# A delta-rule attention whose outputs move from VectorE's recurrence to tiles of 128 tokens on TensorE

## The reference, cut to what matters

```python
def _step(Sm, inputs):                       # Sm: 16x16 per sequence and head
    q_t, k_t, v_t, beta_t = inputs
    Sk = einsum('bhde,bhe->bhd', Sm, k_t)
    delta = v_t - Sk
    Sm = Sm + beta_t[..., None] * einsum('bhd,bhe->bhde', delta, k_t)
    o_t = einsum('bhde,bhe->bhd', Sm, q_t)
    return (Sm, o_t)
# k is divided by its norm; 512 steps, for 16 x 16 = 256 (sequence, head) pairs
x = x + outputs @ Wo + bo
```

## Time and profile before

| what | value |
|---|---|
| three runs | 5764.4, 5775.8, 5776.9 us; median 5775.8 |
| the profiled execution | 5775.2 us, its span 5773.9 us |
| TensorE busy | 3437.4 us (60%), weight loads 2437.2 us (42%) |
| VectorE busy | 4123.4 us (71%) |
| ScalarE busy | 1977.3 us (34%) |
| GpSimd busy | 1477.9 us (26%) |
| TensorE's granted clock, mean | 0.79 of full speed |
| memory traffic | 593.45 MB by DMA, 103 GB/s in the mean |

### The profile page before, as it was taken

One profiled execution on the slowest core, in us unless ns is written; L12 is line 12 of the kernel. 1 busy time (PEld: TensorE's weight loads), 2 busy tenths in 40 slices (PEclk: granted clock), 3 DMA queues, 4 the chain that ended last, 5 costly groups with the idle time before them and its releaser, 6 DMA issues.

```text
span 5773.9 us, 72351 instructions
## 1 busy us (share of the span) xinstructions
PE 3437.4 (60%) x21396; PEld 2437.2 (42%) x21396; DVE 4123.4 (71%) x10439; ACT 1977.3 (34%) x4743; POOL 1477.9 (26%) x1736
## 2 busy tenths in 40 slices
PE   6322153573436534163458888866888589867864
PEld 3101132353314423153436655644666256644654
DVE  1999988999899988998356656664666366655423
ACT  3111021231113311031236555644565255634432
POOL 2010013303451133503450212034000620044334
PEclk8555566796768966597679989978999689978977
DMA  1210001452215511363432334322333243333577
GB/s 48 115 42 6 0 20 47 131 168 71 72 52 168 149 59 57 105 190 115 149 115 87 103 118 127 97 70 96 99 97 91 101 121 98 94 113 119 172 221 210
DMA packets 429264, 593.45 MB, mean 103 GB/s; under 512 B 57680, under 2 KB 304080, under 8 KB 428752
## 3 DMA queue, kind: packets, MB, share of 16 engines
q1 hardware_dynamic: 379728, 454.55, 26.3%
q0 software_dynamic: 49152, 134.28, 7.0%
HBM read 378.89 MB, written 209.72 MB: 102 GB/s over the span
## 4 chain that ended last, share of the span: by engine, by line
DVE 40%; PE 34%; issue 10%; POOL 7%; ACT 4%; DMA 3%; another core or an unknown queue 1%; SPq 1%; DVEq 0%; ACTq 0%; POOLq 0%
PE psum L1019 6%; DVE rec L1083 5%; DVE rec L1085 4%; DVE skb L1088 4%; DVE rec L1096 4%; DVE rec L1099 4%; DVE region L1091 3%; PE psum L929 3%; PE psum L874 3%; PE psum L1027 3%; POOL xbuck L1661 2%; PE psum L913 2%; DVE psum L1201 2%; POOL yg L1671 2%; PE psum L915 2%
## 5 line engine op out<-in xcount | busy, mean ns | idle before, releaser
L1019 PE MATMUL psum<-xgT,w 128*128 128x128 f32 x5376 | 785.7, 293 | 75.3 <-issue 30.1
L1671 POOL DMA_INDIRECT yg<-ybuck,words x512 | 529.6, 1034 | 1122.5 <-issue 643.9
L1019 PEld LDWEIGHTS psum<-xgT,w 128*128 128x128 f32 x5376 | 717.5, 206 | 127.3 <-issue 98.2
L1027 PE MATMUL psum<-w_w2T,hid 128*128 x1344 | 467.5, 432 | 362.3 <-DVE hid L1352 226.4
L1201 DVE CUSTOM_DVE_ANT_0 psum<-psum,xo 128x128 f32<-128x128 f32 (+3 forms) x1024 | 475.6, 520 | 264.2 <-PE psum L895 220.4
L1515 ACT ACTIVATE region<-psum 128x512 f32<-128x512 f32 (+3 forms) x1024 | 415.2, 440 | 524.5 <-PE psum L917 364.3
L806 PE MATMUL psum<-w_ident,xn 128*128 128x128 f32 x512 | 109.9, 354 | 767.8 <-ACT xn L1387 756.8
L1661 POOL DMA_INDIRECT xbuck<-srow,words x512 | 521.6, 1019 | 157.9 <-issue 130.1
L1550 ACT ACTIVATE xgT<-psum 128x256 f32<-128x256 f32 x672 | 256.3, 381 | 725.4 <-PE psum L1009 699.0
L1584 POOL TENSOR_SCALAR small<-small 128x4 f32<-128x4 f32 (+1 forms) x80 | 30.2, 377 | 1620.8 <-DVE small L1050 1619.1
L1370 DVE SCALAR_TENSOR_TENSOR acc<-yg,words,acc 128x256 f32<-128x256 f32 x512 | 251.8, 492 | 266.7 <-DMA yg<-ybuck,words 155.7
(11 more groups left out here) (196 smaller groups left out, 7517.9 us busy)
## 6 DMA issues: line engine op xcount, KB each, us to landing
w<-in_w13T SPq DMA_DIRECT2D x672, 256.0 KB
xg<-xbuck SPq DMA_DIRECT2D x672, 128.0 KB
ybuck<-yrow SPq DMA_DIRECT2D x672, 128.0 KB
xbuck<-x SPq DMA_DIRECT2D x40, 512.0 KB, 5.3
x_scratch<-res SPq DMA_DIRECT2D x64, 256.0 KB
acc<-x_scratch SPq DMA_DIRECT2D x128, 128.0 KB
xbuck<-srow,words POOLq DMA_INDIRECT x512
yg<-ybuck,words POOLq DMA_INDIRECT x512
```

What stands on the lines that cost most here:

```text
L1019: o = e.matmul(psum[:, mi, half], w13[I % 3][:, k, half], xgT[I % 2][:, k, :], start=(k == 0), stop=(k == 1), skip_group_check=True)
L1027: o = e.matmul(psum[:, mi, 0:D], hid[hi][:, 0:128], w2T[:, bass.ds(expert.pop(I), 1), :].rearrange("p a b -> p (a b)"), start=True, stop=True)
L1671: e.indirect_dma_start(yg[y % 5], None, ybuck[g % 2][0:TILES_OF[g] * 128, :], bass.IndirectOffsetOnAxis(ap=posu[g % 2][:, J - ROWS0[g], k: ...
```

## The change

With T the 128 tokens of a quarter, S0 the state at its start and u_s = beta (v - S k), the output is o_t = S0 q_t + the sum over s <= t of (k_s . q_t) u_s. VectorE keeps only the update of S and leaves u_s in `vo`, which `u_turn` turns back as before. TensorE makes the outputs per row of 128 tokens.

In the list of work: queries are projected transposed (`p_q`), each head pair's even and odd half masked with zeros, and written to DRAM; normalized keys are transposed (`k_turn`) and written to DRAM. `first_rows` loads both back (two buffers), takes four banks at once, issues 16 score products over 32 rows of the array each (`a_dots`), multiplies them by the causal triangle on VectorE (`a_mask`), multiplies by u (`a_values`) and adds S0 q, copies four times (`a_out`) and projects with a Wo that is padded to 4 x 128 rows. The rows get a stream of their own, with a rate; the other rates change too. There are 16 load groups instead of 24.

```diff
-HEAD_RATE, TILE_RATE, SUM_RATE, PROJECT_RATE = 0.6, 0.5, 0.2, 0.15
+ROW_RATE, HEAD_RATE, TILE_RATE, SUM_RATE, PROJECT_RATE = 0.45, 0.6, 0.8, 0.3, 0.2
 ...
+                mi, mf = yield from misc.take()
+                put("p_q", n, xi, xt, mi, mf)
+                yield LIGHT
 ...
+            for i in range(4):
+                mi, mf = yield from misc.take()
+                put("k_turn", 4 * k + i, mi, mf)
+                yield LIGHT
+                put("k_out", 4 * k + i, mi)
+                misc.give(mi, "kte", 4 * k + i + 1)
 ...
     def first_rows(q, n):
+        if q and n == 0:
+            put("state_in", q)
         for j in range(4):
             oi, of = yield from xo.take()
+            qi, qf = yield from qkl.take()
+            ti, tf = yield from oT.take()
             nth[f"xo{oi}"] += 16
+            nth[f"ql{qi}"] += 32
             nth["rows"] += 1
             r = nth["rows"]
-            put("o_in", r, q, n, j, oi, of, nth[f"xo{oi}"])
+            put("o_in", r, q, n, j, oi, of, nth[f"xo{oi}"], qi, qf)
+            t_ql = nth[f"ql{qi}"]
+
+            while len(misc.free) < 4:
+                yield LIGHT
+            banks = [misc.get() for _ in range(4)]
+            nth["adot"] += 1
+            t_dot = nth["adot"]
+            put("a_dots", qi, t_ql, banks)
+            yield LIGHT
+            yield LIGHT
+            parts = []
+            for a in range(4):
+                pi, pf = yield from wts.take()
+                nth["amask"] += 1
+                put("a_mask", t_dot, banks[a][0], pi, pf)
+                parts.append(pi)
+                yield LIGHT
+            nth["apv"] += 1
+            t_pv = nth["apv"]
+            put("a_values", q, n, j, qi, nth["amask"], banks, parts)
+            for pi in parts:
+                wts.give(pi, "apv", t_pv)
+            yield LIGHT
+            for a in range(4):
+                nth["aout"] += 1
+                put("a_out", a, t_pv, banks[a][0], ti, tf)
+                misc.give(banks[a][0], "aout", nth["aout"])
+                yield LIGHT
+            qkl.give(qi, "apv", t_pv)
             mi, mf = yield from misc.take()
-            nth["ot"] += 1
-            ot = nth["ot"]
-            put("o_turn", q, n, j, mi, mf)
-            yield LIGHT
-            ci, cf = yield from otc.take()
-            nth["oc"] += 1
-            oc = nth["oc"]
-            put("o_copy", ot, mi, ci, cf)
-            yield LIGHT
             nth["ow"] += 1
             ow = nth["ow"]
-            put("o_proj", oc, mi, ci)
-            otc.give(ci, "ow", ow)
+            put("o_proj", nth["aout"], ti, mi, mf)
+            oT.give(ti, "ow", ow)
 ...
+    def rows():
+        for b in range(4 * (NQ - 1)):
+            while b // 4 not in turned:
+                yield LIGHT
+            yield from first_rows(b // 4, b % 4)
+            shown.add(b)
 ...
+                while b < NB and b not in shown:
+                    yield LIGHT
 ...
-        for i in range(24):
+        for i in range(16):
 ...
+                streams[3].run(ROW_RATE)
                 streams[0].run(HEAD_RATE)
                 streams[1].run(TILE_RATE)
                 streams[2].run(SUM_RATE)
                 ahead.run(PROJECT_RATE)
                 zeros.run(0.2)
-        put("step_out", q)
+        if q + 1 < NQ:
+            put("state", q)
 ...
-    for i in range(4):
-        xo.give(2 + i, "bred", 32)
-    rows = [Strand(first_rows(NQ - 1, n)) for n in range(4)]
-    while not all(t.done for t in rows):
-        for t in rows + streams[1:]:
+    last = [Strand(first_rows(NQ - 1, n)) for n in range(4)]
+    while not all(t.done for t in last):
+        for t in last + streams[:3]:
```

TensorE:

```diff
+            elif name == "p_q":
+                n, xi, xt, mi, mf = u
                 pe.wait_ge(s["xt"], xt)
                 pe.wait_ge(s["d_wA"], 32)
-                pe.wait_ge(s["set"], 4)
+                pe.wait_ge(s[mf[0]], mf[1])
+                for half in range(2):
+                    for k in range(2):
+                        o = e.matmul(psum[:, mi, half * 256:half * 256 + 256], wA[:, k, half * 128:half * 128 + 128],
+                                     blockT[xi][:, k, :], start=(k == 0), stop=(k == 1), skip_group_check=True)
+                o.then_inc(s["pqm"], 1)
 ...
+            elif name == "a_dots":
+                qi, t_ql, banks = u
+                pe.wait_ge(s[f"ql{qi}"], t_ql)
+                for _, mf in banks:
+                    pe.wait_ge(s[mf[0]], mf[1])
+                for c in range(4):
+                    for a, (mi, _) in enumerate(banks):
+                        rows_a = slice(32 * a, 32 * a + 32)
+                        o = e.matmul(psum[:, mi, c * 128:(c + 1) * 128], kTl[qi][rows_a, c // 2, :],
+                                     qTl[qi][rows_a, c % 2, c // 2, :], start=True, stop=True, skip_group_check=True)
+                o.then_inc(s["adot"], 1)
+            elif name == "a_values":
+                q, n, j, qi, t_mask, banks, parts = u
+                pe.wait_ge(s["amask"], t_mask)
                 pe.wait_ge(s["ula"], 4 * q + 2 * (n // 2) + 2)
                 pe.wait_ge(s["uld"], 4 * q + 2 * (n // 2) + 2)
-                pe.wait_ge(s[mf[0]], mf[1])
-                for k in range(2):
-                    o = e.transpose(psum[:, mi, k * 128:(k + 1) * 128], x1[n][:, j, k * 128:(k + 1) * 128], ident[:, :])
-                o.then_inc(s["ot"], 1)
+                for a, (mi, _) in enumerate(banks):
+                    for c in range(4):
+                        hh = 16 * (2 * a + c % 2 + c // 2 * 8)
+                        o = e.matmul(psum[32 * c:32 * c + 16, mi, 0:128], x1[n][:, j, hh:hh + 16],
+                                     wts[parts[a]][:, c, :], start=True, stop=(q == 0), skip_group_check=True)
+                if q:
+                    pe.wait_ge(s["S0"], 16 * q)
+                    for c in range(4):
+                        for a, (mi, _) in enumerate(banks):
+                            rows_a = slice(32 * a, 32 * a + 32)
+                            o = e.matmul(psum[32 * c:32 * c + 16, mi, 0:128],
+                                         S0[rows_a, 2 * (4 * n + j) + c // 2, :], qTl[qi][rows_a, c % 2, c // 2, :],
+                                         start=False, stop=True, skip_group_check=True)
+                o.then_inc(s["apv"], 1)
             elif name == "o_proj":
-                oc, mi, ci = u
-                pe.wait_ge(s["oc"], oc)
-                pe.wait_ge(s["d_set"], 144)
-                for k in range(2):
-                    o = e.matmul(psum[:, mi, 256:512], otc[ci][:, k, :], woA[:, k, :], start=(k == 0), stop=(k == 1))
+                aout, ti, mi, mf = u
+                pe.wait_ge(s["aout"], aout)
+                pe.wait_ge(s["d_set"], 192)
+                pe.wait_ge(s[mf[0]], mf[1])
+                for a in range(4):
+                    o = e.matmul(psum[:, mi, 0:256], oTA[ti][:, a, :], woA[:, a, :], start=(a == 0), stop=(a == 3))
```

VectorE:

```diff
-                c = scan_at(q, t)
-                lag = 2 if t else 0
-                ktt = bc(kq[:, :, t, 0:16], 2, 16)
+                c = scan_at(128 * q + t)
+                kt = bc(kk[:, :, t, :], 2, 16)
                 if third == 0:
                     if t == 0:
-                        dv.wait_ge(s["lda"], 12 * q + 12)
-                        dv.wait_ge(s["ldd"], 12 * q + 12)
+                        dv.wait_ge(s["lda"], 8 * q + 8)
+                        dv.wait_ge(s["ldd"], 8 * q + 8)
                     dv.wait_ge(s["scan"], c)
-                    e.tensor_tensor(tk[:, :, :, :], S[:, :, :, :], ktt, ALU.mult).then_inc(s["scan"], 1)
-                    if t:
-                        e.tensor_tensor(tq[:, :, :, :], S[:, :, :, :], bc(kq[:, :, t - 1, 16:32], 2, 16),
-                                        ALU.mult).then_inc(s["scan"], 1)
+                    e.tensor_tensor(tk[:, :, :, :], S[:, :, :, :], kt, ALU.mult).then_inc(s["scan"], 1)
                     dv.wait_ge(s["scan"], c + 1)
                     e.tensor_reduce(skb[:, :, :], tk[:, :, :, :], AX.X, ALU.add).then_inc(s["scan"], 1)
-                    if t:
-                        dv.wait_ge(s["scan"], c + 2)
-                        e.tensor_reduce(vo[:, :, t - 1, :], tq[:, :, :, :], AX.X, ALU.add).then_inc(s["scan"], 1)
-                    dv.wait_ge(s["scan"], c + 2 + lag // 2)
-                    e.tensor_tensor(ub[:, :, :], vo[:, :, t, :], skb[:, :, :], ALU.subtract).then_inc(s["scan"], 1)
+                    dv.wait_ge(s["scan"], c + 2)
+                    e.tensor_tensor(vo[:, :, t, :], vo[:, :, t, :], skb[:, :, :], ALU.subtract).then_inc(s["scan"], 1)
                 elif third == 1:
-                    dv.wait_ge(s["scan"], c + 3 + lag)
-                    e.tensor_tensor(tk[:, :, :, :], bc(ub[:, :, :], 3, 16), ktt, ALU.mult).then_inc(s["scan"], 1)
+                    dv.wait_ge(s["scan"], c + 3)
```

(50 more changed lines are left out.)

221 lines of the change are left out of this document (136 added, 85 removed).

## The result

| | before | after |
|---|---|---|
| median (runs) | 5770.95 us (8) | 5792.92 us (8) |
| lowest, highest | 5763.3, 5776.9 | 5785.3, 5805.9 |
| profiled execution, its span | 5775.2, 5773.9 us | 5791.7, 5790.4 us |

The account below looks back on a forecast made before the run. VectorE's in-order queue was taken as the bound up to 2705 us. Savings of 481, 6, 14 and 10 against costs of 96, 189, 24, 48, 15, 8 and 91 gave -40 us: 5735 us, range 5600 to 5910.

Parts of the forecast that it names:

- The recurrence: VectorE's steps, one per token: each falls from 4.07 to 3.13 us, -481 us over 512 steps.
- The tiles' faster pace: Expert tiles in quarters 1 to 3: VectorE waits at gates because a tile needs 2.2 us, +189 us.
- Rival (b): Expert tiles follow VectorE at 1.7 us per tile, -126 us, total 5610 us; chance 0.2.
- Row groups beside each other: Score products on TensorE: four row groups overlap as column groups do, so a row's scores take 1.7 us.
- Rival (a): Score products' four row groups run one after another, 4.2 us instead of 1.7, total about 5895 us; chance 0.3.
- Scatters: GpSimd's scatters end some 15 us late before the first gate, half of it hidden: 3 x 8 = +24 us.
- output chain: Rows beside the steps: a chain of 13.4 us against VectorE's 16.1, taken as 1 us wait per row, +48 us.
- The state's 15 us: Reading the state back once per quarter in 64-byte pieces delays the first row's values: 5 us each, +15 us.
- The slack of 2.7 us a row: Beside the steps, VectorE's own 16.1 us per row against the output chain's 13.4, eaten by heads' and projections' matmuls.
- Rival (c): Row phases get quieter, VectorE waiting 10 us per quarter instead of 46, total 5580 us; chance 0.05.
- The tail: Last 16 rows after the recurrence: +109 us for the rows, -18 for sums done meanwhile, +91 us in all.
- The ring: Tail rows: next scores wait for this row's first copy; scores, masks, values and state, copy make 8.6 us a row.

Follow-up runs that it names:

- e5: The changed kernel with the scores' two loops exchanged, so the four matmuls of one row group follow each other: 5773.0 us, 1.0194 of the kernel before.
- e13: The changed kernel without the product of the queries with the carried state and its load, in quarters 1 to 3: 5664.7 us, 0.9996 of the kernel before.
- e12: The changed kernel with loads ahead of the residual's wait, more buffers, no sums between tail rows, q and k stores issued by ScalarE: 5605.9 us, 0.9893 of the kernel before.

## Why the prediction was wrong

By its own steps, on the first chip:

- **The recurrence, right.** 3.13 us a step, quarter 0 427 us (forecast 430). VectorE's busy time in quarters 1 to 3 fell by 97, 93 and 85 us, 276 in all, and the terms for steps, closing pairs, norm sums and masks give 361 + 4 + 7 - 96 = 276. That match is luck: 22 us of the idle time are the spacing between dependent step operations (24 before, 46 after), which the 3.13 us a step include. With it the fall is 254. Counted without what overlaps, the steps gave 379 us (361 forecast); the masks cost 116 (96 forecast: 0.48 us between two steps, near the 0.5 of the sum, but their full 0.69 where they wait), and the gates, which wait now and no longer overlap with a step, 18.
- **The tiles' faster pace, right.** Waits in the tile stretches rose by 174 us (forecast 189), 80 tiles in 176 to 178 us, 2.2 each. Rival (b) falls.
- **Row groups beside each other, right, and dearer to lose than thought.** 1.17 us at full clock, 2.09 at half, forecast 1.7. Values and state, with 3.4 forecast, take 1.65 at full clock: the 0.42 us read for four products held 0.20 that come once, at the change to the next line. Rival (a) falls; its case, run as `e5`, cost 108 us, where (a) had 160 over the forecast.
- **Scatters, output chain, state, too small.** VectorE's idle time in the row stretches rose from 119 to 265 us; less the spacing of the steps, its waits rose by 124, and the three terms were 24 + 48 + 15 = 87. The wait of 1 us a row was right in size: the masks wait 47 us in all. What failed is the scatters' "hides half" and what had no term: the first gates wait 16, 14 and 20 us after the scatters (24 forecast for all three), the norms 22, the choice of experts 17 more than before; adds and layernorm wait 18 less. The state's 15 us don't exist (`e13`). The slack of 2.7 us a row is not one number: `e5` pays 1.4 of 2.3 us more in the chain, `e13` gains 0.1 us a row for 32 instructions less. Rival (c) falls.
- **The tail, the failed step that counts most.** +134 us against +91, the largest miss of a single term. The ring was laid out with the rows bound by their banks; "two buffers let them start a row early, unless SP stands at an earlier wait" names the case that occurred, and the sum did not price it. The residual buffers' cut from six to two was read, but only in what the old tail had. In the traces: 8.6 us a row forecast, 13.5 and then 10 with the blocked loads and the sums, 5.9 without either. The sums' gain after the rows came in (-25 against -18), at a price inside them that was left out.
- **Start and boundaries.** -9 and -17 against -10 for both. The start's +8 did not come; the second part is 12 us shorter, on which there was no term.

The sum: -40, and +22 in VectorE's own work, +37 in the row stretches' waits, +43 in the tail, -15 in the tiles, -28 for start, boundaries and second part, -2 in quarter 0, gives +17; the two profiled executions are 16.5 us apart, the medians 22. A forecast that priced the blocked queue and the sums would have been at "same". Of the signs named beforehand, the tail (377 us, 320 to 345 named), its rows (8 to 16 us apart, 8 to 9 named) and the second part (12 us shorter) showed it wrong; the steps, quarter 0 and VectorE's share in the tile stretches did not.

**The rule weighed.** The prediction read "no cost" from L929 starting 0.15 us after L917, "the spacing of its neighbours". Those neighbours stand behind products of 384 columns. Behind the same L917, of 128 columns, the next product of the same shape starts after 0.06 us, in the kernel before:

```profile
4063.22 0.22 PE L917 MATMUL psum<-identb,maskbb 128*128 128x128 bf16 x1
4063.28 0.33 PE L895 MATMUL psum<-region 128*128 128x384 bf16 x1
```

So that change of shape cost 0.09 us. Instruction by instruction the changed kernel shows the same at a row's changes, at full clock: behind products of 128 columns the first one of another shape starts 0.20 us after the last start and never sooner, where 0.11 us pass without a change; behind 256 columns 0.31 instead of 0.22. (In `e12` the last of L929 starts at 2648.04 and the first of L936 at 2648.25. The view of the chain can't show it: it cuts each piece where the one before ends.) The Trainium skill, TensorEngine Tiling (Array Packing), Tiling Modes, says that changing the mode drains the TensorE. The trace agrees that every change has a price, and it is smaller than the prediction's test of the rule: 4 x 0.1 = 0.4 us a row and not 0.8, at most 6 us in the tail and not 13.

## What to carry to other kernels

In a queue that is taken in order, put a load in front of every wait that it doesn't need. Cutting buffers from six to two turned such a wait into the period of a loop, and no engine's busy share showed it; the chain of waits did. When idle time moves from one stretch to another as rates are changed and the stretches keep their length, the work of the engine that idles doesn't bound them: shorten a chain, don't shift the work (four shifts of work gave +4, +33, +34 and +71 us, two loads and stores taken out of a wait's way -32 and -22). A difference of 0.4% may hold on one chip only.

## What was not expected of the hardware

- 32 score instructions (16 float32 products of 32 rows by 128 columns) take 1.17 us at full clock when neighbouring ones use four different row groups and banks, 2.81 when four in a row use the same group and bank.
- Each change of the weights' shape between 128\*128, 32\*128, 128\*16 and 32\*16 costs about 0.1 us at full clock: the first product of the new shape starts 0.20 us after the last start and not 0.11.
- TensorE's granted clock in the tail's rows was 0.70 with waits of 3 to 5 us for a load in each row and with the sums between them, and 0.91 without either: with the shorter waits the clock rose too (scores 2.09 to 1.2 us, projection 3.4 to 2.0).
- Between two sets of chips the same second part takes 2816 and 2713 us, on a program with one core; quarter 0 is 427 us on both.
